# The row sums of two narrow attentions are carried by ScalarE's transfer queue instead of SyncE's

## What is computed

```python
# layer 0: 16 heads of 16, causal, only the 32 largest scores of each row are kept
vals, idx = top_k(scores, 32);  attn = softmax(masked);  out = attn @ v @ Wo.T + bo
# layer 1: 16 heads of 64, causal softmax attention
probs = softmax(scores + mask); vals = probs @ v @ W_out + b_out
# layer 1's feed-forward: 16 heads of 16, causal softmax, then experts (top 2 of 8, gelu)
att = softmax(where(causal, q @ k.T / 4, -inf)); x = x + (att @ v) @ c_proj_w
x = x + moe_mlp(layernorm(x), router_w, w1, w2)
```

## Time and profile before

| what | value |
|---|---|
| time, median of 3 runs | 6307.12 us (6294.93 to 6309.73) |
| time of the profiled execution | 6296.33 us |
| its span, first to last instruction | 6294.7 us |
| mean granted TensorE clock | 0.877 of full speed |
| DMA queue of the transfers | one (q1), 164.30 MB, 8.3% of 16 engines' span |

### The profile page before, as it was taken

The page is one execution under the profiler, slowest core; times in us unless marked ns, Lnnn a source line. Parts: engine busy times, 40 slices in busy tenths (PEclk is TensorE's granted clock), DMA queues, the critical chain, the costliest instruction groups (busy, mean ns, idle before and its releaser), DMA issues. The chain is left out here.

```text
span 6294.7 us, 84570 instructions
## 1 busy us (share of the span) xinstructions
PE 4972.8 (79%) x31689; PEld 3189.6 (51%) x31689; DVE 4193.8 (67%) x8611; ACT 2791.5 (44%) x5885; POOL 1777.6 (28%) x1429
## 2 busy tenths in 40 slices
PE   4544488897678988888578988889667998997689
PEld 2333346665335655666334654566434664665256
DVE  5999857777786856767686856778677765224421
ACT  2334316663354524655255533566234542552321
POOL 2555503333233402333222421334222430001000
PEclk7566689998789989999689999999779998998899
DMA  2000000000101010000101010000100010001000
GB/s 97 11 11 11 14 34 18 12 17 9 46 16 51 28 52 23 12 12 19 49 16 38 34 59 20 15 12 14 49 21 19 28 36 27 10 15 37 23 28 34
DMA packets 75086, 169.70 MB, mean 27 GB/s; under 512 B 15176, under 2 KB 36528, under 8 KB 71352
## 3 DMA queue, kind: packets, MB, share of 16 engines
q1 hardware_dynamic: 74680, 164.30, 8.3%
HBM read 130.92 MB, written 26.26 MB: 25 GB/s over the span
## 5 line engine op out<-in xcount | busy, mean ns | idle before, releaser
L1373 DVE MAX8 vals<-work 128x8 f32<-128x128 f32 (+7 forms) x1536 | 1080.9, 744 | 0.6
L1718 POOL TENSOR_SCALAR keep<-ssb,vals 128x128 bf16<-128x128 f32 (+7 forms) x512 | 876.4, 1724 | 0.0
L1705 POOL TENSOR_TENSOR pool_step<-ones 128x2 f32<-128x2 f32 x256 | 49.9, 195 | 2592.4 <-DVE vals L1373 2592.2
L1387 DVE MATCH_REPLACE8 work<-vals,work 128x128 f32<-128x128 f32 (+7 forms) x1024 | 751.0, 739 | 0.0
L428 PE MATMUL ring<-ident,pr 128*128 128x128 f32 x2304 | 467.8, 321 | 352.6 <-POOL pr L1723 331.0
L535 PE MATMUL pA<-SC 128*128 128x512 f32 (+3 forms) x1536 | 624.3, 516 | 124.7 <-ACT SC L1125 103.3
L1072 ACT ACTIVATE prT<-ring 128x512 f32<-128x512 f32 (+1 forms) x768 | 379.4, 495 | 662.0 <-PE ring L428 661.1
L1723 POOL TENSOR_TENSOR pr<-keep,pr 128x128 f32<-128x128 bf16 (+7 forms) x512 | 648.4, 1289 | 0.0
L1502 DVE TENSOR_REDUCE nmax<-pA 128x1 f32<-128x1024 f32 (+7 forms) x512 | 382.2, 750 | 306.4 <-PE pA L536 295.2
L428 PEld LDWEIGHTS ring<-ident,pr 128*128 128x128 f32 x2304 | 325.6, 165 | 488.5 <-POOL pr L1723 357.2
L723 PE MATMUL pA<-hT,SC 128*128 128x512 f32 x1024 | 494.4, 606 | 0.0
(11 more groups left out here) (198 smaller groups left out, 8676.7 us busy)
## 6 DMA issues: line engine op xcount, KB each, us to landing
SC<-in_w SPq DMA_DIRECT2D x64, 512.0 KB, 4.4
parts<-SC SPq DMA_DIRECT2D x72, 256.0 KB, 2.4
SC<-in_wqkv SPq DMA_DIRECT2D x32, 384.0 KB, 2.9
stage<-parts SPq DMA_DIRECT2D x64, 192.0 KB
SC<-parts SPq DMA_DIRECT2D x24, 384.0 KB
stage<-parts SPq DMA_DIRECT2D x64, 128.0 KB
SC<-in_ffn_we SPq DMA_DIRECT2D x4, 2048.0 KB, 10.2
SC<-in_wqkv SPq DMA_DIRECT2D x8, 768.0 KB, 7.5
```

What stands on the lines that cost most here:

```text
L1373: m = v.max(vals0[:, y, i, 8 * n:8 * n + 8], src[:, lo:hi])
L1387: done[i] = cht.mark(v.match_replace(out=work0[:, lo:hi], in_to_replace=vals0[:, y, i, 8 * n:8 * n + 8], in_values=src[:, lo:hi], imm_valu ...
L1718: pool.tensor_scalar(keep0[:, lo:hi], ssb0[:, p % 2, lo:hi], vals0[:, p % 2, i, TOPK - 1:TOPK], None, ALU.is_ge).then_inc(s["k"], 1)
```

## The change

The two functions `sums_columns` leave SP's stream and enter ACT's. What they transfer, their semaphores and what waits for these stay as they were. In attention 0 they stand at the same tick, in front of ACT's exponentials of that tick. They wait for ACT's own copy. In attention 2 they stand behind the four exponentials of n == 2 (on SP it was n == 3), and the last one behind the last copy out of PSUM.

```diff
@@ SP, topk
-                def sums_columns(g):
-                    emptied(("v", b, 16 * g + 15))
-                    for j in range(4):
-                        sp.dma_start(rsb0[32 * g + 8 * j:32 * g + 8 * j + 8, :],
-                                     oall0[32 * j + 16:32 * j + 17, g, :]).then_inc(s["sd"], 16)
-                    if r == 2 and p >= 18 and (p - 18) % 16 == 0:
-                        sums_columns((p - 18) // 16)
@@ SP, flip
-                def sums_columns(g):
-                    sp.wait_ge(s["o"], (b * G + g) * 2 + 2)
-                    for j in range(4):
-                        sp.dma_start(rsb2[32 * g + 8 * j:32 * g + 8 * j + 8, :], oall2[g][32 * j + 16:32 * j + 17, :])\
-                          .then_inc(s["sd"], 16)
-                        if n == 3 and g:
-                            sums_columns(g - 1)
-                sums_columns(G - 1)
@@ ACT, topk
+                def sums_columns(g):
+                    act.wait_ge(s_re, place["v", b, 16 * g + 15] + 1)
+                    for j in range(4):
+                        act.dma_start(rsb0[32 * g + 8 * j:32 * g + 8 * j + 8, :],
+                                      oall0[32 * j + 16:32 * j + 17, g, :]).then_inc(s["sd"], 16)
+                    if r == 2 and p >= 18 and (p - 18) % 16 == 0:
+                        sums_columns((p - 18) // 16)
                     if r == 2 and 0 <= p - 1 < 64:
                         exponentials(p - 1)
@@ ACT, flip
+                def sums_columns(g):
+                    act.wait_ge(s["o"], (b * FL.GROUPS + g) * 2 + 2)
+                    for j in range(4):
+                        act.dma_start(rsb2[32 * g + 8 * j:32 * g + 8 * j + 8, :],
+                                      oall2[g][32 * j + 16:32 * j + 17, :]).then_inc(s["sd"], 16)
+                        if n == 2 and g:
+                            sums_columns(g - 1)
                         if n == 9 and g + 1 < FL.GROUPS:
                             rows_high(g + 1)
                 out_of_psum(FL.GROUPS - 1, 1)
+                sums_columns(FL.GROUPS - 1)
```

## The result

The changed kernel takes 6228.16 us (median of 4 runs, 6224.33 to 6236.83). The kernel before took 6305.7 us beside it, and the ratio is 0.9887 (95% interval 0.9873 to 0.9901): 1.1% faster. The profiled execution took 6224.38 us with a span of 6222.7 us, 72.0 us under the span before. The forecast was 6250, that is 57.3 us less than the profiled execution before.

The account below looks back on a forecast made before the run. No engine bounds it throughout; DVE's reciprocals wait for row sums queued behind 3 MB of staging. 75.3 + 12.6 - 30.6 = 57.3 us off 6296.33 gives 6239.0; the median stands 10.8 above, so 6250, range 6222 to 6282.

Parts of the forecast that it names:

- The three long waits: Start of flip, batches 0 to 2: reciprocals on time, then maxima rows held by the drain; 75.3 us gained.
- Batch 3, group 1: Attention 2's reciprocal no longer waits for sums held by the third group's staging; 12.6 us gained.
- ACT's cost: Four issues take ACT 2.68 us; over 24 places 30.6 us lost, between 0 and 64.3.
- Beside "wide": Three places where exponentials of both attentions queue behind ACT's issues; 2 us each, 6 lost.
- Beside "moe": Six places where ACT's issues come before the gelu; 1 us each, 6 lost.
- "Flip" with top-k: Nine places where ACT's issues come ahead of the next exponentials; 4.1 us a batch, 12.3 lost.
- Flip of batch 3: Three places: ACT free late, 1.2 us twice and 2.7 in group 3; 5.1 lost.
- First top-k: Three places with ACT idle before and after; 0.4 us each, 1.2 lost.
- A: Beside flip's staging: ACT's issues squeeze between SP's, done only at about 1625; 6261 us, chance 0.23.
- B: At the drain: sums on ACT's queue land no earlier, gains zero, costs stay; 6338 us, chance 0.05.
- C: All issue places: no cost of ACT is absorbed, 64.3 in place of 30.6; 6284 us, chance 0.10.
- D: Start of flip: maxima rows not held by the drain, 92.1 in place of 75.3; 6233 us, chance 0.12.

Follow-up runs that it names:

- e6: Changed kernel with flip's staging halved, the third group's six transfers put behind the maxima rows; 6193.2 us, ratio 0.9837 to the kernel before.
- e3: Kernel before with only the sums of attention 2 moved to ACT, those of attention 0 kept on SP; 6296.9 us, ratio 0.9995.
- e1: Kernel before with only attention 0's second group of sums (p = 34) moved to ACT; 6217.4 us, ratio 0.9879.
- e4: Changed kernel with ACT issuing the sums of p = 34 four ticks later, amid the staging's drain; 6246.1 us, ratio 0.9917 to the kernel before.
- e7: Changed kernel with the first group's two maxima rows in flip also issued by ACT, staging as before; 6205.5 us, ratio 0.9852 to the kernel before.
- e10: Kernel before, all sums on SP: staging halved, one transfer a group, fourth group's staging behind the first group's sums; 6163.6 us, ratio 0.9790.
- e8: Changed kernel with one transfer on ACT for each group's sums instead of four; 6192.3 us, ratio 0.9828 to the kernel before.
- e9: Kernel before with one transfer on SP for each group's sums instead of four; 6275.8 us, ratio 0.9966.
- e5: Kernel before, sums on SP, with flip's staging halved, the third group's six transfers put behind the maxima rows; 6203.0 us, ratio 0.9848.

## Why the prediction was right, and where it was off

**The three long waits: right, 82.6 us against 75.3, and the difference is luck.** The reciprocals are on time, and what is late next is the maxima rows. The prediction had SP issue the low row at 1644.4, T0 + 45.4, and the drain hold PE until T0 + 50.1. In the changed kernel SP issues it at T0 + 45.8, and PE starts at T0 + 48.9. With the drain taken away (e6) L658 starts 27.8, 27.5 and 36.8 us earlier than before, 92.1 in all, which is the prediction's upper bound. So the drain holds back 9.6 us in the changed kernel (1.5 + 5.6 + 2.5), where 16.8 were forecast (92.1 - 75.3), 11.6 of them in batch 2 by its long drain. That the number came out higher is the drains' doing: batch 2's took 58.5 us in the profiled execution before and held L658 only to 49.8 after, 8.7 us that the change didn't bring. Without that it is 73.9. Batch 1's ran the other way, 53.1 us against 49.5.

**Batch 3, group 1: right.** 12.6 forecast. The shift against the kernel before grows from -61.13 us at SP's issue of group 1's low maxima row to -74.91 at that reciprocal, 13.8.

**ACT's cost: too high in sum, and wrong in its parts.** Forecast 30.6. By place:
- Beside "wide" 6 was forecast, and 3.6 + 3.6 + 3.8 = 11.0 are lost across the three sites. The table's +14.6 has 3.6 more, of which e3 shows 2.3 without any place there; in batch 0 PE is busy 374.7 us between the marks, in batches 1 and 2 371.8 and 371.7. Of the five terms this one was set too low: the exponentials of both attentions are queued behind the issues, and PE came late in its turn (the 1.58 us in the row of 1274.98).
- Beside "moe" 6 was forecast. It is 1.0, with 1.7 in e1, which moved nothing there: no cost.
- "Flip" with top-k 12.3 was forecast. From the start of L658 on the three flips lose 2.5 + 1.5 + 3.6 = 7.6 us against before, of which 2.7 are longer busy time of PE; in e3 it is 10.5 with 3.0. They gave the 46.1 us of waits above. (e1, with none of attention 2's issues on ACT, wins 6.0 there, but its PE is busy 14.7 us less than the changed kernel's, so it can't serve as the measure.)
- Flip of batch 3: 5.1 forecast, 3.0 measured (-74.9 to -72.0).
- First top-k: 1.2 forecast, nothing seen.

Summed, 11.0 + 0 + 7.6 + 3.0 is 21.6, 9.0 less than forecast. With it 82.6 + 13.8 - 21.6 = 74.8 us should have come off, and 72.0 did; the difference is of the size of the 3.6 beside "wide". So the forecast of 57.3 was 14.7 too low against the spans, about half by the costs and half by the long waits' luck.

**The rivals.** A is out: ACT's single issues took 0.63 to 0.66 us while SP's took up to 4.96 in the changed kernel's batch 0 and 13.33 in e4's batch 1. B is out by e4 and e7. (At its threshold the prediction calls 30.9 less than the costs; it is 0.3 more than 30.6, which changes nothing.) C is out, since moe costs nothing. D, that the maxima rows are not held, is out as well: e6, where they are not, has D's 92.1 us, and the changed kernel has 82.6.

**Open.** What sets the granted clock behind L658, 0.92 in one execution and 0.88 in the other of the two rows above, these runs don't show; it moves as much time as some of the steps compared here. The profile also leaves some 3 to 7 us of e10's lead behind L658 unexplained. And the gain of e8 is 36 us by medians, 26 by spans; with the 8.1 us of longer drains added, the spans come to 34.

## What to carry to other kernels

A small transfer that something waits for must not stand behind megabytes on its queue: halve what is ahead of it and put the rest behind, before giving it to another engine's queue. A compute engine pays for every issue in its own stream (2.6 us for four), so move only the places where the long wait is, and make one transfer of four first. When a wait is taken away, ask both what its engine still has to do before the next link and which queue that link stands in: here the two ended within 1.5 to 5.6 us of each other. And before a few microseconds between two profiles are credited to a change, compare PE's busy time for the same matmuls and the lengths of the drains: here these differed by up to 14 us over three flips and 9 us in one batch.

## What the runs showed of the hardware

- An issue by ScalarE takes 0.63 to 0.66 us and holds its stream for that long. It is not lengthened by SP's being stuck: in e4 ACT issues in 0.65 us inside one SP issue of 13.33 us.
- In a drain of 3 MB on SP's queue, the low maxima row on ScalarE's queue lands 4.0 to 6.4 us after its issue (e7) and the sums 4.6 to 6.0 us after their last one (e4). On SP's queue behind it they take 20.7 (the sums, before) and 22.7 (the row, changed kernel). With half the staging ahead and near its end, SP's row takes 1.8 to 2.6 (e6).
- One transfer over four rows of partitions issues in 0.56 to 0.60 us, no longer than each of the four that it replaces. Right behind SP's twelve staging issues it took up to 2.06 us (e9).
- Six staging issues take 3.9 us (e5), twelve take 24.6 (before): beyond the first seven, which took 4.6 us in the changed kernel's batch 0, single ones take up to 4.96.
